# Node stage of a graph network kernel: two small operations of each step go from VectorE to GpSimd, one of them a step later

## The reference, cut to what matters

```python
H = X @ W                                   # [10000, 512] @ [512, 512]
msgs = H[src] * norm[:, None]
out = segment_sum(msgs, dst) + b            # self loops included
x = _layernorm(x + where(out >= 0, out, 0.01 * out))   # per row, eps 1e-5
```

## Time and profile before

| | |
|---|---|
| median of 3 runs | 1352.58 us (1351.42 to 1354.11) |
| span of the profiled execution | 1351.3 us |
| busy, of the whole span | TensorE 1282.1 (95%), VectorE 1075.9 (80%), ScalarE 638.2 (47%), GpSimd 817.3 (60%) |
| node stage | about 180 to 448 us |
| busy in 180 to 448 us | TensorE 265.5, VectorE 244.6, ScalarE 209.3, GpSimd 177.1 us |

### The profile page before, as it was taken

How to read it: one execution, slowest core, us unless ns; L and a number is a source line. 1 busy time by engine, 2 the same in 40 slices (tenths; PEclk the granted TensorE clock), 3 DMA queues, 4 the chain that set the end, 5 groups by cost and what they waited for, 6 DMA issues and landing times. The chain is left out here.

```text
span 1351.3 us, 21818 instructions
## 1 busy us (share of the span) xinstructions
PE 1282.1 (95%) x6374; PEld 1029.1 (76%) x6374; DVE 1075.9 (80%) x2074; ACT 638.2 (47%) x1243; POOL 817.3 (60%) x752
## 2 busy tenths in 40 slices
PE   7989989999999699999999999999999999979887
PEld 5768768888888588888888888888888888754333
DVE  6577649999999225888889988888888888977887
ACT  3576637888888212333233223322332233257777
POOL 3667346776765542566655666666666565467775
PEclk9999989999999799999999999999999999879999
DMA  8889767888885514444444344444444443759886
GB/s 279 287 280 297 259 203 261 255 257 276 259 261 188 187 47 110 141 131 129 97 135 128 127 126 131 139 135 137 133 140 140 140 140 94 258 175 368 272 283 228
DMA packets 128299, 257.93 MB, mean 191 GB/s; under 512 B 21459, under 2 KB 21907, under 8 KB 128114
## 3 DMA queue, kind: packets, MB, share of 16 engines
q1 hardware_dynamic: 97490, 175.31, 39.8%
q0 software_dynamic: 29920, 80.38, 20.6%
q10 hardware_dynamic: 832, 1.57, 0.3%
HBM read 197.18 MB, written 73.60 MB: 200 GB/s over the span
## 5 line engine op out<-in xcount | busy, mean ns | idle before, releaser
L208 PE MATMUL ps<-w_lo,w_hi 128*128 128x512 f32 (+2 forms) x1140 | 416.3, 365 | 3.6 <-DVE w_lo L1430 1.4
L210 PE MATMUL ps<-w_hi 128*128 128x512 f32 (+2 forms) x1140 | 410.7, 360 | 0.0
L209 PE MATMUL ps<-w_hi,w_lo 128*128 128x512 f32 (+2 forms) x1140 | 410.2, 360 | 0.0
L208 PEld LDWEIGHTS ps<-w_lo,w_hi 128*128 128x128 f32 x1140 | 217.5, 191 | 36.1 <-DVE w_lo L1512 1.9
L210 PEld LDWEIGHTS ps<-w_hi 128*128 128x128 f32 x1140 | 217.0, 190 | 32.4
L209 PEld LDWEIGHTS ps<-w_hi,w_lo 128*128 128x128 f32 x1140 | 217.8, 191 | 29.8
L1268 POOL TENSOR_TENSOR acc_x<-acc_x,node_rows 128x512 f32<-128x512 f32 x72 | 114.8, 1594 | 85.8 <-DMA node_rows<-x_table 81.5
L923 POOL TENSOR_TENSOR node_y<-node_z,node_x 128x512 f32<-128x512 f32 x79 | 102.7, 1300 | 74.0 <-DVE node_agg L1021 39.5
L208 PE MATMUL ps<-w_lo,agg_hi 128*128 128x512 f32 x316 | 132.8, 420 | 1.1 <-DVE agg_lo L992 1.1
L210 PE MATMUL ps<-w_hi,agg_hi 128*128 128x512 f32 x316 | 125.7, 398 | 0.0
L209 PE MATMUL ps<-w_hi,agg_lo 128*128 128x512 f32 x316 | 125.2, 396 | 0.0
(11 more groups left out here) (271 smaller groups left out, 2878.7 us busy)
## 6 DMA issues: line engine op xcount, KB each, us to landing
node_x<-in_x SPq DMA_DIRECT2D x79, 256.0 KB, 4.1
x_table<-node_x SPq DMA_DIRECT2D x79, 256.0 KB, 2.4
node_rows<-x_table SPq DMA_DIRECT2D x79, 256.0 KB, 8.4
coef_all<-coef_table SPq DMA_DIRECT2D x38, 512.0 KB, 7.6
edge_part<-part SPq DMA_DIRECT2D x40, 256.0 KB, 4.4
out_dram<-rows_over_w_lo SPq DMA_DIRECT2D x40, 256.0 KB, 5.7
node_x<-in_ea SPq DMA_DIRECT2D x38, 256.0 KB, 4.3
msg_table<-dst_rows_and_msg SPq DMA_DIRECT2D x38, 256.0 KB, 5.0
```

The costliest lines, as they stand in the source:

```text
L208: pe.matmul(to, left[0], right[1], start=first, stop=False, skip_group_check=onto)
L209: pe.matmul(to, left[1], right[0], start=False, stop=False, skip_group_check=onto)
L210: return pe.matmul(to, left[0], right[0], start=False, stop=last, skip_group_check=onto)
```

## The change

VectorE no longer forms the bias (L1014) nor the low half of the weight pieces (L1024). GpSimd does both. In step j of its loop it now runs: the bias of tile j-10 (VectorE made that of tile j-9 in the same step), y of tile j-6, the gather for tile j+2, and the low half of piece j. Its loop is four steps longer, so that all 79 biases are made. The bias signals a semaphore of its own, `shift_ok`, and ScalarE's x1 of tile j-10 waits for it instead of the second count of `scale_ok`. The edge stage gets a wait of TensorE for all low halves.

```diff
     def gpsimd_program(pool):
 
-        for j in range(-2, NT + 6):
+        def split_piece(j):
+            if has_piece(j):
+                pool.wait_ge(g.w_hi_ok, j - FIRST_PIECE + EARLY + 1)
+                nc.gpsimd.tensor_tensor(piece(g.w_lo, j), piece(g.over_lo, j), piece(g.w_hi, j).bitcast(F32), ALU.subtract).then_inc(g.w_lo_ok, 1)
+
+        for j in range(-2, NT + 10):
+            i = j - 10
+            if i >= 0:
+                m = i % RY
+                pool.wait_ge(scale_ok, i + 1)
+                nc.gpsimd.tensor_scalar(mv[:, m, 3:4], mv[:, m, 0:1], mv[:, m, 2:3], -1.0, ALU.mult, ALU.mult).then_inc(shift_ok, 1)
             i = j - 6
-            if i >= 0:
+            if 0 <= i < NT:
                 pool.wait_ge(leaky_ok, i + 1)
                 pool.wait_ge(agg_ok, min(i + 5, NT))
                 wait(pool, x1_ok, i - RY + 1)
...
+            split_piece(j)
...
             if on(10):
                 q = (s - 10) % RY
-                act.wait_ge(scale_ok, 2 * (j - 10) + 2)
+                act.wait_ge(shift_ok, j - 9)
...
-            if on(9):
-                dve.wait_ge(scale_ok, 2 * (j - 9) + 1)
-                v.tensor_scalar(mv[:, m9, 3:4], mv[:, m9, 0:1], mv[:, m9, 2:3], -1.0, ALU.mult, ALU.mult).then_inc(scale_ok, 1)
...
-            if has_piece(j):
-                dve.wait_ge(g.w_hi_ok, j - FIRST_PIECE + EARLY + 1)
-                v.tensor_tensor(piece(g.w_lo, j), piece(g.over_lo, j), piece(g.w_hi, j).bitcast(F32), ALU.subtract).then_inc(g.w_lo_ok, 1)
...
                 pe.wait_ge(bias_step, BIAS_SPLIT)
+                pe.wait_ge(g.w_lo_ok, EARLY + (2 * NW - EARLY) * WH // PIECE)
```

More of the change, by code:

```diff
@@ L878, in node_stage @@
         turned, hi_ok, lo_ok, mm_ok = (sem(n) for n in ("node_turned", "node_high", "node_low", "node_product"))
-        z_ok, leaky_ok, y_ok, stat_ok, root_ok, scale_ok, x1_ok = (sem(n) for n in (
-            "node_z_ok", "node_leaky", "node_y_ok", "node_stat", "node_root_ok", "node_scale", "x1_ok"))
+        z_ok, leaky_ok, y_ok, stat_ok, root_ok, scale_ok, shift_ok, x1_ok = (sem(n) for n in (
+            "node_z_ok", "node_leaky", "node_y_ok", "node_stat", "node_root_ok", "node_scale", "node_shift", "x1_ok"))
         x1_out = g.x1_out = [sem(f"x1_out{s}") for s in range(RY)]
```

## The result

The changed kernel takes 1418.56 us (median, 1416.71 to 1422.52) against 1352.26 us for the kernel before in the same comparison: a ratio of 1.0485, 95% interval 1.0466 to 1.0504. The forecast was 1417. The profiled execution has a span of 1420.0 us.

The account below looks back on a forecast made before the run. The prediction took TensorE to bound the node stage at 3.24 us per step. Rounds of 3.73, then 61 of 4.21 us, put y of step 77 +62.4 later; with the last steps +64, 1352.6 + 64 = 1417 us, range 1395 to 1455.

Parts of the forecast that it names:

- The closed round: Node stage, each step: bias, x1, y, gather and piece wait for each other in turn, 4.21 us against TensorE's 3.24.
- The low end of the range: All prices at their lowest (bias 0.12, signal 0.05, piece 0.33): y of step 77 at 467.4, in all 1395 us.
- The far bound of 0.81: GpSimd to ScalarE signal: a copy-to-gather wait of 0.81 us, taken as no measure; 0.10 used instead.
- The second ring: Two-step round through x1, z, high half, VectorE's aggregate, y, gather, piece, bias: 8.3 us, 4.16 per step, nearly level.
- The way along the steps: Forecast starts of y in the node stage: step 10 at 207.82, step 16 at 230.20, step 77 at 487.0 us.
- Steps without a piece: Node stage, steps 10 to 16: the one-step round without the piece on GpSimd, 3.73 us each.
- VectorE's relief worth nothing: VectorE loses 0.38 us per step beside a TensorE never idle; at most 2.5 us could return over the stage.
- rival D: VectorE was the hidden bound and the new work fits GpSimd's idle time: at most 2.5 us gained, 1350; chance 0.05.
- Rival B: Bias or piece on GpSimd also collides with VectorE's aggregate: 0.3 to 0.6 us more per step, 1447 us; chance 0.11.
- Rival C: TensorE, idle 1 us in 4.2, is granted a lower clock in the node stage: 1431 us and more; chance 0.04.
- What would show it: Signs: y spaced about 4.2 us, ScalarE idle before x1 for the bias, stage 60 us longer, TensorE busy some 77%.

Follow-up runs that it names:

- y_eight: The changed kernel with eight buffers of y instead of four, so y no longer waits for x1 of its own step: 1423.33 us, ratio 1.0524.
- bias_sooner: The changed kernel with GpSimd making the bias of tile j-9 instead of j-10 in step j, at the same place: 1353.69 us, ratio 0.9997.
- x1_later: The changed kernel with eight buffers of y and ScalarE making x1 (and SP storing it) one step later: 1354.61 us, ratio 1.0005.
- bias_back: The changed kernel with the bias returned to VectorE and the piece left on GpSimd: 1353.2 us, ratio 1.0002.
- bias_after_y: The changed kernel with GpSimd making the bias of tile j-9 right behind y, ahead of the gather: 1360.92 us, ratio 1.0050.
- piece_back: The changed kernel with the piece returned to VectorE and the bias left on GpSimd: 1401.26 us, ratio 1.0352.
- bias_before_piece: The changed kernel with GpSimd making the bias of tile j-9 behind the gather and the piece last: 1400.71 us, ratio 1.0344.
- bias_twice: The changed kernel with each bias computed twice on GpSimd, first into a spare tile: 1456.18 us, ratio 1.0745.

## Why the prediction was right

Point by point, by its own steps.

*The closed round.* Forecast 4.21 us with a piece; measured 4.17 to 4.21 in 39 of the 61 steps, with 4.18 in the step shown. Its terms in the step shown: bias and hand-over 0.30 for 0.32 (the operation was 0.05 longer, the hand-over 0.07 shorter), x1 0.82 and the way back 0.17 as said, y to gather 1.42 for 1.45, gather 1.03 for 0.97, piece 0.44 to the next start for 0.48. The errors of 0.02 to 0.07 nearly cancel, which is partly luck. That the interpolation from the 512 columns and the one-column copy gave 0.48, with 0.47 recorded, is what made the size right; a quarter of the 512 (0.33) would have given 9 us less. The low end of the range holds a slip: its terms lead to 467.7 for y of step 77, not 467.4, and the 1.5 us of the last steps are missing there, so it should have been 1397 instead of 1395. The far bound of 0.81 for the hand-over the earlier trace rows was rightly put aside.

*The second ring.* It was called nearly level, and it was: 0.18 us in the step shown. But the sum goes by the first alone, and y_eight shows that the loss is not its alone: with it open the second takes over at 4.36 us per step. The loss goes only where both are opened (bias_sooner, x1_later, bias_back) or made short (bias_after_y). No run opens the second and leaves the first.

*The way along the steps.* y of step 10 was forecast at 207.82 and started at 207.28, y of step 16 at 230.20 and 230.50, y of step 77 at 487.0 and 489.66. That step 10 came out within 0.5 us is luck: the profiled execution was 1.0 us ahead from the start (its first y at 192.43, before 193.44), and the first bias of all met the aggregate and lasted 0.79 instead of 0.27. Of the 2.7 us at the end 0.3 stood there at step 16, and 2.3 come from three steps of 4.48, 4.71 and 5.75 us. The 4.71 from y of step 16 to y of step 17 is shown: the bias started at 233.40, 0.01 us behind the aggregate, and lasted 0.79. In the 5.75 us that end at 299.93, from step 31 to step 32, the gather started 1.2 us late, and the piece behind it then met the aggregate (0.86 us). The gather of the same step in the kernel before, and then in the changed one:

```profile
278.08 0.98 POOL L927 DMA_INDIRECT node_sum<-sum_table,last_edge  x1 [1.18 <-ACT node_x L971]
```

```profile
296.67 1.02 POOL L937 DMA_INDIRECT node_sum<-sum_table,last_edge  x1 [1.21 <-issue]
```

It is as late in both, so the change did not bring this delay; why it is there stays open. In the kernel before that step took 3.48 us instead of 3.24; in the closed ring the delay costs its full length. Step 31 is the longest in piece_back (5.37), bias_before_piece (5.34) and bias_twice (5.98) too. Steps 78 to 84 took 21.0 us against 19.4, the 1.5 more that were said. In all +66.6 at the end of the stage for +64.

*Steps without a piece.* Here a term was off: 3.73 was forecast, 3.87 measured (from step 10 to 16, 23.22 us over 6), with y waiting for the aggregate. The second ring is the longer one there. The prediction priced it only with a piece in it. It cost 0.8 us.

*VectorE's relief worth nothing.* bias_back and bias_sooner bear it out, with 0.20 and 0.38 us less work per step and ratios of 1.0002 and 0.9997. Their intervals of about 0.2% are too wide to rule out the at most 2.5 us of rival D, but the stage is no shorter in their traces: y of step 10 to y of step 84 takes 236.6 and 237.7 us, before 236.7. The shape of D (the work hides, no difference) is what bias_sooner runs; it needed the lag of the bias to be another.

*Rival B.* Right as a mechanism and right that it stood close by. The trace has it in a few steps of the changed kernel (biases of 0.79, 0.79 and 0.50, one piece of 0.86), in bias_twice in 41 of 61 steps at about 0.5 us each, and in y_eight in about every second. bias_sooner and x1_later have such meetings too and lose nothing, so a meeting costs only in a ring that sets the pace. By the Trainium skill (SBUF — State Buffer, section SBUF: two separate sides) the one that starts first holds the pair for its whole instruction and the other blocks. The bias that started 0.02 us behind an aggregate in bias_twice agrees with that: it took 0.78 us. The bias that started 0.05 us ahead agrees only in part: it took its 0.26 us, but the aggregate kept its 0.75 beside it and did not wait for its end.

*Rival C.* The granted clock stayed at 1.00 in the 61 steps. TensorE was busy in 82% of them, not in 77%: per step some matmul of it runs during 3.51 us where it was 3.24, though the mean length of one is as before (396 and 395 ns for L210 and L209). My reading, which no run tests, is that they overlap less when TensorE has to wait between groups.

*What would show it.* The chain was said to show as ScalarE's idle time before x1, put down to the bias: 115.2 us. It did.

## What to carry to other kernels

When work moves to an engine with idle time, look first at what the new place closes: follow the result to its reader, and from there through every wait for a buffer back to the engine that makes it, counting steps. A ring of one step sets the pace as soon as its length is above that of the busiest engine, however idle its engines are. Here 0.27 us on an engine with a third of its time free cost 48 us (piece_back), and in the changed kernel one index took the whole loss away (bias_sooner). Then look for the next ring: opening the first alone gained nothing (y_eight). The index is not enough either, as the place in the engine's list counts with it (bias_before_piece against bias_sooner). Idle time of an engine that follows another can be used for work that nobody in the ring waits for (the piece in bias_back), or for work that stands far enough ahead of its reader.

## What the runs showed of the hardware

An operation of one column on GpSimd took 0.26 us when it started 0.05 us ahead of VectorE's 512 column operation on two SBUF inputs, and 0.78 us when it started 0.02 us behind. A piece of 128 columns took 0.47 us alone and 0.85 us when it started 0.22 us behind such an operation. VectorE's operation kept its 0.75 us in all of these. In other meetings it did not: it took 1.03 us when a piece started at the same time (bias_back, 304.67 us, the piece 0.47), and 1.07 us when a piece started 0.73 us behind it (bias_sooner, 237.50 us, the piece 0.65). In the last case both were longer than alone; why stays open. What I had not expected is that so small an operation is hit by all of it: a shift of 0.07 us in the order of two starts moves a step by half a microsecond. The hand-over from GpSimd to ScalarE took 0.03 us, that from ScalarE to GpSimd 0.17.
